# Attention on one Trainium2 core: TensorE's waits of a unit collected ahead of its first transpose

## What is computed

```python
# first attention: 32 heads of 128, 8 groups of 4 heads, 768 keys (512 of the cache, 256 new)
scores = jnp.einsum('bhld,bhtd->bhlt', qh, k_full) / math.sqrt(HD)
attn = jax.nn.softmax(scores, axis=-1)
out = jnp.einsum('bhlt,bhtd->bhld', attn, v_full)
return out.transpose(0, 2, 1, 3).reshape(b, l, NH * HD) @ wo.T
...
# cross attention: 16 heads of 96, 4 groups of 4 heads, 768 keys (512 context, 256 own)
scores = jnp.einsum('bkgqd,bksd->bkgqs', q, k) * scale
attn = jax.nn.softmax(scores.astype(jnp.float32), axis=-1).astype(q.dtype)
out = jnp.einsum('bkgqs,bksd->bkgqd', attn, v)
```

## Time and profile before

| | |
|---|---|
| median of three runs | 1362.09 us |
| the profiled execution | 1362.19 us, span 1360.4 us |
| granted TensorE clock, mean over the span | 0.936 |
| TensorE matmuls (PE) | 1159.0 us busy, 85% |
| TensorE weight loads (PEld) | 879.0 us busy, 65% |
| VectorE (DVE) | 942.6 us busy, 69% |
| ScalarE (ACT) | 528.1 us busy, 39% |
| GpSimd (POOL) | 556.8 us busy, 41% |

### The profile page before, as it was taken

How to read it: one execution, slowest core, us unless ns; L and a number is a source line. 1 busy time by engine, 2 the same in 40 slices (tenths; PEclk the granted TensorE clock), 3 DMA queues, 4 the chain that set the end, 5 groups by cost and what they waited for, 6 DMA issues and landing times.

```text
span 1360.4 us, 16919 instructions
## 1 busy us (share of the span) xinstructions
PE 1159.0 (85%) x5660; PEld 879.0 (65%) x5660; DVE 942.6 (69%) x1483; ACT 528.1 (39%) x1042; POOL 556.8 (41%) x382
## 2 busy tenths in 40 slices
PE   4939622668799999999999999879799999987999
PEld 2413311227487878787878787755587888875887
DVE  7998999976577777777777777645355555543543
ACT  1211210222465555555555555532353444342111
POOL 3774531310255555555555554420454544441000
PEclk9968955788999999999999999988999999999899
DMA  7172442001100101010101000151001000001122
GB/s 285 63 232 89 151 170 70 24 0 48 57 24 20 55 20 54 19 54 19 54 19 53 20 31 12 55 163 24 6 13 28 20 9 20 1 24 62 35 99 84
DMA packets 38834, 77.70 MB, mean 57 GB/s; under 512 B 11395, under 2 KB 19588, under 8 KB 35588
## 3 DMA queue, kind: packets, MB, share of 16 engines
q1 hardware_dynamic: 37188, 71.86, 16.1%
q0 software_dynamic: 1600, 5.24, 1.2%
HBM read 69.75 MB, written 9.44 MB: 58 GB/s over the span
## 4 chain that ended last, share of the span: by engine, by line
PE 66%; DVE 23%; issue 7%; ACT 3%; POOL 1%; DMA 0%; DVEq 0%; POOLq 0%; ACTq 0%
PE PS L1427 14%; PE PS L1425 14%; PE PS L1426 14%; PE PS L1491 9%; PE PS L1465 5%; DVE nmax L1103 3%; PE PS L1342 2%; DVE PTL L1144 2%; DVE blkamax L909 1%; PE PS L1596 1%; DVE QTH L1096 1%; PE PS L1290 1%; PE PS L1274 1%; DVE QTL L1098 1%; PE PS L1393 1%
## 5 line engine op out<-in xcount | busy, mean ns | idle before, releaser
L561 POOL TENSOR_TENSOR arena<-arena,rsum 128x768 f32<-128x768 f32 x192 | 285.3, 1486 | 466.7 <-DVE rsum L1108 466.7
L1103 DVE TENSOR_REDUCE nmax<-PS 128x1 f32<-128x768 f32 x192 | 183.3, 955 | 195.3 <-PE PS L1427 194.0
L729 ACT ACTIVATE arena<-PS,nmax 128x768 f32<-128x768 f32 x192 | 173.4, 903 | 270.1 <-DVE nmax L1103 270.0
L1491 PE MATMUL PS<-identf,arena 128*128 128x128 f32 x1152 | 160.2, 275 | 32.5 <-DVE PTL L1144 19.8
L1491 PEld LDWEIGHTS PS<-identf,arena 128*128 128x128 f32 x1152 | 133.8, 140 | 70.3 <-issue 46.4
L1144 DVE TENSOR_TENSOR PTL<-PS,PTH 128x384 fp32r<-128x384 f32 x256 | 129.7, 548 | 1.8 <-ACT PTH L745 1.1
L745 ACT ACTIVATE PTH<-PS 128x384 fp32r<-128x384 f32 x256 | 111.6, 488 | 37.7 <-PE PS L1491 34.5
L1465 PE MATMUL PS<-arena 128*96 128x256 f32 x384 | 87.5, 379 | 0.0
L1098 DVE TENSOR_TENSOR QTL<-arena,QTH 128x512 fp32r<-128x512 f32 (+1 forms) x48 | 79.3, 1653 | 1.7
L1425 PE MATMUL PS<-WOH,OTH 128*128 128x512 f32 (+1 forms) x192 | 76.6, 399 | 4.1 <-DVE OTL L1121 3.0
L544 POOL TENSOR_TENSOR WQL<-arena,WQH 128x512 fp32r<-128x512 f32 (+1 forms) x48 | 57.7, 1205 | 49.9 <-ACT WQH L614 49.9
(11 more groups left out here) (242 smaller groups left out, 2543.6 us busy)
## 6 DMA issues: line engine op xcount, KB each, us to landing
arena<-in_wq SPq DMA_DIRECT2D x32, 256.0 KB, 2.6
arena<-in_wo SPq DMA_DIRECT2D x8, 1024.0 KB, 4.9
arena<-in_expert_w SPq DMA_DIRECT2D x8, 1024.0 KB, 4.8
arena<-in_wgu SPq DMA_DIRECT2D x11, 512.0 KB, 3.9
arena<-v_dram SPq DMA_DIRECT2D x8, 384.0 KB, 3.4
arena<-in_wq SPq DMA_DIRECT2D x16, 192.0 KB, 2.9
arena<-in_wo SPq DMA_DIRECT2D x4, 768.0 KB, 5.6
arena<-in_wd SPq DMA_DIRECT2D x4, 704.0 KB, 4.0
```

The source lines that it names most:

```text
L561: pool.tensor_tensor(PR[:, u % 4, :], PR[:, u % 4, :], rsum[:, u % 4:u % 4 + 1].broadcast_to([P, KEYS]), ALU.mult).then_inc(s["pn_ready"], 1)
L729: act.activation(PR[:, slot, :], SC[pair][:, 0:KEYS], ACT.Exp, bias=nmax[:, slot:slot + 1], accum_out=psum_exp[:, slot:slot + 1]).then_inc ...
L1103: dve.tensor_reduce(nmax[:, slot:slot + 1], SC[pair][:, 0:KEYS], AX.X, ALU.max, negate=True)\
L1491: mm = pe.transpose(bank(B_PT[half])[:, k * P:(k + 1) * P], PR[:, u % 4, c * P:(c + 1) * P], identf[:])
```

## The change

All waits of a unit now come ahead of its first transpose: q_ready in the units that have it, exp_done, pt_out0, pt_out1 and last pn_ready. The condition under which there are scores to make is computed first and used twice. In the last two units of the last group exp_done is now also waited for; before it was not waited for inside the unit. The instructions that compute and what they signal stay as they were.

```diff
@@ -1483,18 +1483,20 @@
                     for u in range(UNITS):
                         U = UNITS * g + u
 
+                        next_scores = not (last and u >= UNITS - 2)
+                        if next_scores and u % RT == 2:
+                            pe.wait_ge(s["q_ready"], KPAIRS + GH * g + u // RT + 2)
+                        pe.wait_ge(s["exp_done"], U + 1)
+                        pe.wait_ge(s["pt_out0"], U)
+                        pe.wait_ge(s["pt_out1"], U)
                         pe.wait_ge(s["pn_ready"], U + 1)
                         for half in range(2):
-                            pe.wait_ge(s[("pt_out0", "pt_out1")[half]], U)
                             for k in range(3):
                                 c = 3 * half + k
                                 mm = pe.transpose(bank(B_PT[half])[:, k * P:(k + 1) * P],
                                                   PR[:, u % 4, c * P:(c + 1) * P], identf[:])
                             mm.then_inc(s["pt_psum"], 1)
-                        if not (last and u >= UNITS - 2):
-                            pe.wait_ge(s["exp_done"], U + 1)
-                            if u % RT == 2:
-                                pe.wait_ge(s["q_ready"], KPAIRS + GH * g + u // RT + 2)
+                        if next_scores:
                             if u < UNITS - 2:
                                 scores(g, U + 2, u + 2, u % 2)
                             else:
```

## The result

The changed kernel takes 1394.95 us (median of 4 runs, 1394.19 to 1395.43), the kernel before beside it 1362.07: a ratio of 1.0246, interval 1.0224 to 1.0269. The forecast was 1381.3, its range ended at 1388. It is slower, for the most part by the mechanism forecast, and by 14 us more. The profiled execution took 1394.89 with a span of 1393.1, 32.7 over the span before.

What follows compares the result with a forecast made beforehand. TensorE was taken as the bound, busy 66.6 of 68.0 us in a middle pass, idling for VectorE. First attention 13.2 + 2.6 + 3.3 = 19.1 us, all else 0: 1362.2 + 19.1 = 1381.3 us, range 1372 to 1388.

Steps and rivals of the forecast that it cites:

- exp_done and q_ready: Moving these two waits ahead of a unit's first transpose was to cost nothing, covered by a lead of 4.6 us.
- The border between transposes and scores: Dropping the waits between a unit's transposes and scores was to give back at most 0.01 us a unit, taken as 0.
- pt_out1 ahead of the first transpose: First attention: transposes start 0.14 us after VectorE's second subtraction, costing 2.2 us a middle pass and 19.1 us in all.
- rival 1: Only units that wait today pay for the moved pt_out1 wait: 27 x 0.38 = 10.3 us, 1372.5 us; chance 0.07.
- the unknown: Where the pt_out1 wait rides ahead of the first transpose: 0.11 us taken; 0.06 gives 3.5 us less, another 0.05 3.5 more.
- The units that I let off: First attention: unit 14's loss absorbed, taken as 0; units 8 and 11 taken as 0.25 us each instead of 0.32.
- The clock falls: Idle stretches in first and last group grow from 1.6 to 2.1 us; four falls give 8 us, 1389; chance 0.07.
- The second attention: pt_out1 leads by 2.0 us there, so the change was to cost 0, at most 0.6 us over its 12 waits.
- What would show it: Signs in the trace: TensorE's 27 waits for VectorE's subtraction rise to over 60, and from 19.8 us to about 40.
- The pass of 70.5 us: Sign in the first attention: a middle pass, 68.33 us before, was to take about 70.5 us.

Runs made afterwards that it cites:

- pt_out1 back: Changed kernel with the pt_out1 wait put back between the third and fourth transpose, its other waits still collected: 1363.63 us, ratio 1.0003.
- the control with fillers: Kernel before plus six never-read matmuls behind units 2, 3, 4 of the first group and 8, 11 of the last, first attention only: 1361.84 us, ratio 0.9998.
- The filler runs: Changed kernel plus six never-read matmuls behind some units of first and last groups: 1394.9 us in both attentions, 1387.64 us in the first attention only.

## Why the prediction was wrong in size

*exp_done and q_ready: nothing.* Right: 1.0003 with them collected and pt_out1 back, and pt_out1 alone (1.0164) equals all collected with pt_out1 last (1.0173).

*The border between transposes and scores: nothing.* Right: the changed kernel has no wait there and gains nothing from it.

*pt_out1 ahead of the first transpose: the start is the second subtraction's end plus 0.14.* This is the step that failed: the term was of the right kind and too small. Units 0, 4, 7, 8, 10, 11, 13, 14, 15 all start late by it, also those that started at once before (unit 7 grows a pass by 0.27 to 0.31), so rival 1 is out. But 0.14 was 0.24 to 0.25. I had named the place of the wait as the unknown, priced one more step at 0.05, the difference of the two delays in the earlier trace rows, and put +3.5 us on it. Its price is the 0.106 between the starts of two waiting steps, and it came to 7.6 us in the first attention (changed kernel against pt_out1 last). Both rows of mine showed a late wait with no step behind it (pt_out0 in the last step, pt_out1 on the fourth load), so neither bounded this case from above. With pt_out1 last, the delay is 0.14 as taken.

*The units that I let off.* Unit 14 was to be absorbed by unit 15. With the delay as forecast (pt_out1 last), 14 and 15 together pay 0.49 instead of 0.39, units 8 and 11 0.32 each instead of 0.25 (the 0.32 that I worked out and shaded down); units 4 and 0, net of their shorter transposes, pay 0.40 and 0.33 for the 0.38 of each. A pass pays 2.4 instead of 2.2, six passes 1.2 us more. Over the attention I put it at 1.7, which is what the other terms leave.

*The clock.* "The clock falls" had a chance of 0.07 and 8 us for four falls. It happened, with four falls and 6.6 us, and with pt_out1 last too, so it would have come at the delay forecast. I had the idle stretches right (2.1 to 2.2 us, three in a row) and set against them only that the clock held at 1.6 in one execution. That says nothing of 2.2, and little of 1.6, where the control with fillers had it fall. Added matmuls alone brought the clock back to 1.00 (0.92 without them over the first group). The Trainium skill (TensorE: Matmul & The Clock Gate, Part 1) says that the ratio of the clock is set by how busy TensorE has been lately. By that rule the work between the waits counts as well as the waits. The filler runs fit it but do not separate the two, since the fillers shortened the stretches and added work at once.

*The second attention: nothing.* Right in itself. Behind pt_out0's copy the first transpose now starts 0.10 instead of 0.15 later, as pt_out0 stands in the last step:

```profile
1056.27 0.55 DVE L1150 COPY arena<-PS 128x384 f32<-128x384 f32 x1
...
1056.92 0.85 PE L1496 MATMUL PS<-identf,arena 128*128 128x128 f32 x6 [0.18 <-issue]
```

The sum: 19.1 forecast + 7.6 (delay) + 1.7 (units let off, the remainder) + 6.6 (clock) = 35.0 in the first attention, as in the table (8.0 + 19.7 + 7.3). By these terms the delay alone would have given 1388.9, just past the end of the range, and the clock alone 1387.9. Outside the first attention it is -2.3, mostly phases of the clock between the attentions, which no run here varied on purpose. Why they shift stays open.

*What would show it.* "About 40 us" of waits was right (39.3, though in 51 waits and not over 60), and that was luck: the waits leave out the 6.6 us lost at half speed, and in units that had no idle time a matmul's modelled end reaches 0.16 past its pitch (0.40 and 0.24 in the earlier trace rows) and hides as much of each new wait. The pass of 70.5 us was 71.58; with pt_out1 last, 70.76.

## What to carry to other kernels

Every wait ahead of an instruction holds all that stands behind it on the engine: put the latest one as far back as it can go, and work that needs none of them in front (here -2.3%, where collecting cost +2.5%). Where several waits must stand together, the latest of them goes where no other step follows it; the same four waits in another order were worth 0.7%. And when an idle stretch is to grow, count the clock as a cost of its own beside the stretch's length, and do not take one execution in which it held as proof.

## What the runs showed of the hardware

In these traces the waits ahead of the transposes stand in steps of TensorE's sequencer with one or two waits each, and one more rides on the weight load. From a late semaphore to the first transpose it was 0.04 to 0.05 us on the load with the steps passed (written-out groups with pt_out1 first; six transposes then take 0.87), 0.09 to 0.10 as the second wait of the last step (pt_out0 in the second attention), 0.14 as its first or only wait (kernel before; pt_out1 written last), and 0.24 to 0.25 with one more step behind it. Which place a wait gets follows from the order in which they are written, and was another in the looped passes than in the written-out groups when pt_out1 stood first.

TensorE's clock fell to 1.2 GHz in the first attention where units stood idle for 2.2 us one after another (changed kernel), for 2.07 (pt_out1 last, pt_out1 alone) and for 1.98 (pt_out1 first). A single stretch of 2.18 passed at 1.00 (unit 6 of the last group, with fillers). In the second attention it fell behind stretches of 1.75 (pt_out1 first), 1.72 (pt_out1 back), 1.67 (changed kernel) and 1.61 (kernel before with fillers), while in the kernel before it held through three of 1.61 in a row. Eighteen extra matmuls shortened the group that it fell in by 3.6 us.
